# Attention scores of a two-layer decoder from two 12-bit pieces in one-pass matmuls of 32 rows, four heads at once, with maxima added by PE and dense fillers in the loops

## The reference

```python
# layer 0, x: (8, 128, 128), 16 heads of 8
q = q * cos + rotate_half(q) * sin          # 16 wide: two halves of 8
k = k * cos + rotate_half(k) * sin
attn1 = jnp.einsum('bhid,bhjd->bhij', q1, k1) * scale
attn2 = jnp.einsum('bhid,bhjd->bhij', q2, k2) * scale
probs = jax.nn.softmax(attn1, axis=-1) - lam * jax.nn.softmax(attn2, axis=-1)
out = jnp.einsum('bhij,bhjd->bhid', probs, v)          # v is 16 wide
# layer 1, 16 heads of 8, causal
score = jnp.einsum('bhsd,bhtd->bhst', q, k)
attn = jax.nn.softmax(jnp.where(causal, score, -inf) / sqrt(8), axis=-1)
y = jnp.einsum('bhst,bhtd->bhsd', attn, v)
```

## Time and profile before

| | |
|---|---|
| median of 3 runs | 631.55 us (631.34 to 631.91) |
| the profiled execution | 630.57 us, its span 628.8 us |
| mean granted clock of PE | 0.825 |
| busy, share of the span | PE 88%, DVE 43%, ACT 36%, POOL 13% |
| DMA | 31.66 MB, mean 50 GB/s |

### The profile page before, as it was taken

One profiled execution on the slowest core, in us unless ns is written; L12 is line 12 of the kernel. 1 busy time (PEld: TensorE's weight loads), 2 busy tenths in 40 slices (PEclk: granted clock), 3 DMA queues, 4 the chain that ended last, 5 costly groups with the idle time before them and its releaser, 6 DMA issues.

```text
span 628.8 us, 12335 instructions
## 1 busy us (share of the span) xinstructions
PE 553.6 (88%) x4854; PEld 401.8 (64%) x4854; DVE 272.6 (43%) x679; ACT 223.5 (36%) x406; POOL 84.0 (13%) x131
## 2 busy tenths in 40 slices
PE   8658999999886899828999859999999899999994
PEld 3446777777664389415566636677777667677764
DVE  4333444442147643503243359666672325223325
ACT  1202433433323142000245426665665062443340
POOL 4000111111131000200000044322222100000001
PEclk9755555555588699955599979999999998999998
DMA  7522221200303000122110000000100000111110
GB/s 224 199 102 100 89 71 69 74 33 2 134 1 134 1 2 2 40 96 100 68 39 24 34 11 10 13 11 11 44 1 1 1 25 23 46 34 34 35 41 33
DMA packets 22637, 31.66 MB, mean 50 GB/s; under 512 B 5428, under 2 KB 13956, under 8 KB 22336
## 3 DMA queue, kind: packets, MB, share of 16 engines
q1 hardware_dynamic: 22592, 31.01, 14.7%
HBM read 26.68 MB, written 4.12 MB: 49 GB/s over the span
## 4 chain that ended last, share of the span: by engine, by line
PE 76%; DVE 12%; DMA 6%; ACT 3%; issue 1%; POOL 1%; SPq 0%; POOLq 0%; DVEq 0%; ACTq 0%
PE ps L563 16%; PE ps L942 9%; PE ps L925 9%; PE ps L585 7%; PE ps L841 4%; PE ps L558 4%; PE ps L598 3%; PE ps L814 2%; PE ps L913 2%; DMA near<-stacks 2%; DMA stacks<-arena 2%; PE ps L822 2%; PE ps L830 2%; PE ps L749 2%; PE ps L783 2%; PE ps L864 2%
## 5 line engine op out<-in xcount | busy, mean ns | idle before, releaser
L1241 DVE TENSOR_REDUCE negm<-ps 128x4 f32<-128x512 f32 x96 | 61.9, 686 | 124.1 <-PE ps L563 124.1
L990 ACT ACTIVATE probs<-ps 128x512 f32<-128x512 f32 (+1 forms) x100 | 56.5, 590 | 97.6 <-PE ps L563 97.2
L563 PE MATMUL ps<-near 8*128 8x128 f32 (+1 forms) x768 | 76.7, 420 | 13.0 <-DMA near<-stacks 6.9
L563 PEld LDWEIGHTS ps<-near 8*128 8x128 f32 (+1 forms) x768 | 65.9, 309 | 28.5 <-issue 22.8
L563 PE MATMUL ps<-w1a 8*128 8x128 f32 (+1 forms) x768 | 69.4, 385 | 0.0
L942 PEld LDWEIGHTS ps<-w1a,arena 128*128 128x128 f32 x512 | 61.0, 196 | 7.2 <-issue 6.2
L990 ACT ACTIVATE arena<-ps,w1a 128x512 f32<-128x512 f32 x64 | 43.4, 687 | 60.6 <-PE ps L925 59.4
L563 PEld LDWEIGHTS ps<-w1a 8*128 8x128 f32 (+1 forms) x768 | 59.2, 277 | 8.4 <-issue 8.4
L1550 DVE SCALAR_TENSOR_TENSOR racc<-ps,sm,racc 128x128 f32<-128x128 f32 x128 | 36.0, 344 | 64.7 <-PE ps L942 64.6
L942 PE MATMUL ps<-w1a,arena 128*128 128x128 f32 x512 | 61.4, 280 | 0.8 <-DVE racc L1541 0.8
L925 PE MATMUL ps<-xT,w1a 128*128 128x512 f32 x128 | 57.9, 594 | 1.4 <-ACT xT L990 1.4
(11 more groups left out here) (180 smaller groups left out, 725.3 us busy)
## 6 DMA issues: line engine op xcount, KB each, us to landing
near<-stacks SPq DMA_DIRECT2D x24, 256.0 KB
w1a<-stacks SPq DMA_DIRECT2D x24, 256.0 KB
stacks<-arena SPq DMA_DIRECT2D x6, 512.0 KB
w1a<-in_w1a SPq DMA_DIRECT2D x1, 2048.0 KB, 7.7
w2a<-in_w2a SPq DMA_DIRECT2D x1, 2048.0 KB, 7.8
w1a<-in_w1b SPq DMA_DIRECT2D x16, 128.0 KB, 2.0
w1a<-in_w2b SPq DMA_DIRECT2D x16, 128.0 KB, 2.1
con<-in_con SPq DMA_DIRECT2D x1, 644.0 KB, 5.7
```

The costliest lines, as they stand in the source:

```text
L563: last = mm(o[:, cols], left[rows, cols], right[rows, cols], start=not causal, stop=not causal or k == 3)
L990: return nc.scalar.activation(o, i, f, **kw)
L1241: nc.vector.tensor_reduce(negm[:, n % 2, 4 * g:4 * g + 4], tiles(bank(RING_S[(4 * n + g) % 3]), 4, P), AX.X, ALU.max, negate=True).then_in ...
```

## The change

Queries and keys are split on DVE and POOL into a high piece (the bits kept by `HEAD_BITS`) and the rest. Two pieces of the queries times two of the keys times 8 dimensions make 32 rows of contraction, stored to and loaded from DRAM accordingly; the operands get the type float32r, for which a matmul is one instruction. A unit v is now four heads of four batches of one half (`place`): 16 units and 8 units as before, with 16 tiles each. The loads of a unit are three DMAs (one for keys, two for queries) and not two, in other lists, and the move of the maxima by DMA is gone: DVE and POOL split the maxima too (`high_maxima`, `split_maxima`), PE transposes the pieces, ACT copies them to `mT` (128 partitions), and for each turned tile a second float32r matmul of 32 rows adds them, with `pick` as weights. Three fillers of 512 columns stand in each step ahead of the first half of `head_values`; the fillers in front of the loops grow from 6 to 8 and from 18 to 30. The two softmaxes of the first attention are now combined in its second half of units, in POOL operations of 256 elements instead of 128.

The core of the diff:

```diff
-MROW = HD
+PIECES = 2
+HEAD_BITS = -4096
 RING = 8
-AHEAD = FLIGHT = 4
-LOADS = 2
+LOADS = 3
...
+            def load_stacks(a, v, count):
+                c, m, half = place(v, count)
+                at = 4 * HD * m * ROW + (2 * c + half) * HALF
+                slot, signal = v % RING, a.stack[v % RING]
+                sp.dma_start(keys_of[slot].bitcast(F32), bass.AP(stacks, KEYS + 4 * HD * m * ROW + at, [[ROW, 8 * HD], [0, 2], [1, HALF]])
+                             ).then_inc(signal, 16)
+                for p in range(PIECES):
+                    sp.dma_start(queries_of[slot][p:P:2, :].bitcast(F32), bass.AP(stacks, p * P * ROW + at, [[ROW, 4 * HD], [0, 2], [1, HALF]])
+                                 ).then_inc(signal, 16)
-                    sp.dma_start(tile, bass.AP(stacks, (t * NH + h) * HEAD, [[HALF, 4], [ROW, QUAD], [1, HALF]])
-                                 ).then_inc(a.stack[h % FLIGHT], 16)
-            def move_maxima(a, n, slot):
-                sp.wait_ge(a.mc, n + 1)
-                sp.dma_start(queries_of[slot][MROW:MROW + 3 * QUAD + 1:QUAD, :], mT[:, n % 2, :]
-                             ).then_inc(a.mrow[n % FLIGHT], 16)
...
+            def low_piece(a, n, turn):
+                pool.wait_ge(a.hi, turn)
+                nc.gpsimd.tensor_tensor(rope[:, 2 * n, :], rope[:, 2 * n, :], rope[:, 2 * n + 1, :], ALU.subtract
+                                        ).then_inc(a.qlo, 1)
+            def split_maxima(a, v):
+                pool.wait_ge(a.mhi, v + 1)
+                nc.gpsimd.tensor_tensor(mparts[:, v % 2, :, 16:32], over(negm[:, v % 2, :], 4), mparts[:, v % 2, :, 0:16],
+                                        ALU.subtract).then_inc(a.msplit, 1)
...
                 for k in range(4):
                     cols = slice(k * P, (k + 1) * P)
-                    for o, left, right, g, depth, _, done in cells:
-                        rows = slice(QUAD * g, QUAD * g + depth)
-                        last = mm(o[:, cols], left[rows, cols], right[rows, cols], start=not causal, stop=not causal or k == 3)
-                        if k == 3:
+                    for o, left, right, g, shift, _, done in cells:
+                        rows = slice(QUAD * g, QUAD * g + QUAD)
+                        last = mm(o[:, cols], left[rows, cols], right[rows, cols], start=not causal,
+                                  stop=shift is None and (not causal or k == 3))
+                        if k == 3 and shift is None:
                             last.then_inc(done, 1)
+                    for o, left, right, g, shift, _, done in cells:
+                        if shift is not None:
+                            rows = slice(QUAD * g, QUAD * g + QUAD)
+                            last = mm(o[:, cols], pick[rows, k, :], shift[rows, :], start=False, stop=not causal or k == 3)
+                            if k == 3:
+                                last.then_inc(done, 1)
...
             def head_maxima(a, n):
-                pe.wait_ge(a.max, 4 * n + 4)
+                pe.wait_ge(a.msplit, n + 1)
...
-            def head_values(a, n, pair, c):
+            def head_values(a, n, part):
...
+                    keep_busy(3, BANK_V)
...
                     if turned:
-                        pe.wait_ge(a.mrow[n % FLIGHT], (a.turns + n // FLIGHT + 1) * 16)
+                        pe.wait_ge(a.mc, n + 1)
...
-            keep_busy(6, BANK_M0)
+            keep_busy(8, BANK_M0)
...
-            keep_busy(18, BANK_M0)
+            keep_busy(30, BANK_M0)
...
+                def high_maxima(n):
+                    dve.wait_ge(a.max, 4 * n + 4)
+                    if n >= 2:
+                        dve.wait_ge(a.mt, n - 1)
+                    ts(mparts[:, n % 2, :, 0:16].bitcast(I32), over(negm[:, n % 2, :], 4).bitcast(I32), HEAD_BITS, None,
+                       ALU.bitwise_and).then_inc(a.mhi, 1)
...
                     if n >= 2:
                         finish_head(n - 2, n % 2)
+                    if 0 <= n + 2 < count:
+                        high_maxima(n + 2)
```

More of the change, by code:

```diff
@@ L18 @@
 BF16 = mybir.dt.bfloat16
+F32R = mybir.dt.float32r
+I32 = mybir.dt.int32
 ALU = mybir.AluOpType
@@ L128, in decoder_kernel @@
         rw0 = sb("rw0", [P, E0])
+        with nc.sbuf_tensor("late", [P, 2, 4, HALF], F32R) as late:
+            pass
         w1a = sb("w1a", [P, E0, F0 * P])
@@ L137, in decoder_kernel @@
         rw1, rb1, b2s = sb("rw1", [P, E1]), sb("rb1", [P, E1]), sb("b2s", [E1, P])
-        near = sb("near", [P, 2, 4, HALF])
-        late = w1a[:].rearrange("p e f -> p (e f)").rearrange("p (k s t) -> p k s t", k=2, s=4)
+        near = sb("near", [P, 2, 4, HALF], F32R)
+        pick = sb("pick", [P, 4, P], F32R)
         probs = sb("probs", [P, 2, 16, P])
@@ L336, in heads @@
[L336 to L349, removed]
@@ L363, in _ @@
             load(w2a[:], d["w2a"], ld_f)
[L364 to L369, removed]
+            for p, (queries, keys) in enumerate(((D.hi, D.hi), (D.qlo, D.klo))):
+                sp.wait_ge(queries, 1)
+                sp.dma_start(bass.AP(stacks, p * P * ROW, [[T, P], [1, T]]), rope[:, 1 - p, :]).then_inc(D.kept, 16)
+                sp.wait_ge(keys, 2 - p)
+                sp.dma_start(bass.AP(stacks, KEYS + p * ROW, [[2 * ROW, PAIRS * HD], [T, 2], [1, T]]), rope[:, 3 - p, :]
+                             ).then_inc(D.kept, 16)
+            sp.wait_ge(D.kept, 16 * 4)
+            heads(D, 0, PAIRS, PAIRS)
             def weights(pair, slot):
@@ new lines, in heads @@
+            def heads(a, count):
+                pool.wait_ge(a.vall, 4 if a is A else 2)
+                split_maxima(a, 0)
+                split_maxima(a, 1)
+                for n in range(count + 2):
+                    if n < count:
+                        if n >= 2:
+                            pool.wait_ge(a.pv, n - 1)
+                        values(a, n, count)
+                    if n + 2 < count:
+                        split_maxima(a, n + 2)
+                    if a is A and n - 2 >= NH // 2:
+                        add_outputs(n - 2)
@@ L615, in step @@
                     if 0 <= n - 1 < count:
-                        head_values(a, n - 1, pair, 0)
+                        head_values(a, n - 1, 0)
                     scored = n + 3 < count
@@ L622, in step @@
                     if 0 <= n - 1 < count:
-                        head_values(a, n - 1, pair, 1)
+                        head_values(a, n - 1, 1)
                     if 0 <= n + 2 < count:
@@ L1056, in _ @@
                 values(g)
+            act.wait_ge(lam_sum, 1)
+            fn(lams[:, 2:4], lams[:, 0:2], ACT.Exp).then_inc(lam_exp, 1)
+            act.wait_ge(ld_p, 16)
+            fn(pick[:], pick_in, ACT.Copy).then_inc(tables, 1)
             for half in range(2):
@@ L1324, in _ @@
             rotate(2)
-            sum_keys(2)
+            dch.wait()
+            dve.wait_ge(A.mul, 3)
+            link(tt(rope[:, 4, :], rope[:, 4, :], rope[:, 5, :], ALU.subtract))
+            high_piece(A, 2)
+            dve.wait_ge(A.full, 1)
+            high_piece(A, 0)
+            low_keys(A, 2, 1)
             rotate(3)
-            sum_keys(3)
+            dve.wait_ge(A.full, 2)
+            high_piece(A, 1)
             dve.wait_ge(ld_l, 16 * 6)
```

238 lines of the change are left out of this document (135 added, 103 removed).

## The result

| | before | changed |
|---|---|---|
| median | 631.73 us (631.34 to 641.25, 4 runs) | 579.37 us (579.21 to 582.12, 4 runs) |
| ratio | | 0.9183, 95% interval 0.9149 to 0.9218 |
| profiled span | 628.8 us | 577.6 us |
| mean granted clock | 0.825 | 0.919 |

The change made the kernel 52 us faster. The forecast was 563 (548 to 606), its likeliest case's own range 553 to 578, so the measured time lies just above that range and inside the wide one. The clock rose in both loops, as that case had it, but 16 us of its gain of 68 did not come. Executions more than 1.5% over the quickest one of the same kernel count as slow and are left out of every ratio here.

What follows compares the result with a forecast made beforehand. PE was taken to bound both head loops. From the profiled 630.6 us, 55.5 came off in the first loop and 13 in the second, giving 562, so 563 us in the median; range 548 to 606.

Steps and rivals of the forecast that it cites:

- likeliest case: Whole kernel: clock up in both loops, score calls of 0.66 to 1.10 us, 553 to 578 us; chance 0.60.
- What bounds: Both head loops: PE alone bounds the steps, full for 7.40 us in the first, with DVE 3.53 and ACT 3.03.
- the rival of an engine other than PE: Steps: DVE, POOL and ACT bound them at about 5.0 to 5.2 us, +10 to 573 us; chance 0.09.
- A float32r matmul: Score calls: 0.85 us instead of 1.10 at the high clock level, 1.3 instead of 2.02 at the low one.
- The clock: Both loops: rises to the high level within the first two steps and stays up; full steps 4.4 us in the first.
- both misses: Within the forecast's range: calls 0.25 us longer cost +8 us, the clock rising two steps later +6 us.
- Start: First loop: loads ready at 31.2, first scores at 31.5, ramp of 8 us, turned scores at 39.5, against 50.81: -11.3 us.
- Second loop: Masks start 4.2 us earlier, ramp -6.0, steps 0 and 1 -3.5, later steps +0.7: sum -13 us.
- one-pass matmuls run one behind another: Score calls: 1152 matmuls not beside each other, at 57 ns instead of 35, +25 to 588 us; chance 0.05.
- a float32r tile is as long as a whole f32 tile: Score calls: 2.0 us each, +1.15 for some 36 calls, +41 to 605 us; chance 0.10.
- the slower case of 112 ns each: Score calls: float32r tiles neither overlap nor are shorter than f32 instructions, +89 to 652 us; chance 0.03.
- The clock staying down in the first loop: First loop: low clock level throughout, steps of 7.4 us again, 604 us; chance 0.08.

Runs made afterwards that it cites:

- Run 8: Changed kernel with each score matmul of the queries' side written twice in the first loop, 32 instead of 24 per full call: 582.32 us.
- run 1: Changed kernel without the three fillers in each step: 607.65 us, ratio to before 0.959.
- run 9: Changed kernel with fillers behind score calls in ramps and first steps, 58 instead of 30 ahead of the second loop, none in later full steps: 546.77 us.
- run 3: Changed kernel with rows of float32r and bf16 test matmuls replacing the 30 fillers ahead of the second loop: 585.04 us, no comparison.
- run 2: Kernel before the change with the same three fillers added in each step: 609.71 us, ratio 0.9621.
- run 12: Kernel before the change with the fillers of run 9, 46 instead of 18 ahead of the second loop: 635.04 us, ratio 0.9951.
- run 4: Changed kernel with three more fillers behind every score call of both ramps and 58 instead of 30 ahead of the second loop: 568.79 us.
- run 5: The kernel of run 4 without the three fillers in the steps of the second loop: 562.97 us, ratio 0.8862.

## Why the prediction came out as it did

- **What bounds** (right). PE is full in every window of full steps, before and after; DVE has 3.3 a step and ACT 2.9. The hop over POOL stays hidden, the rival of an engine other than PE fell.
- **A float32r matmul** (the mis-sized term). I took "0.85" for a call at the high level "nearest for the pace of instructions", inside bounds of 0.66 and 1.10; it is 1.04, and 1.90 at the low level against my 1.3. Run 8 shows why the pace of 34 ns was the wrong row: it is what four row groups make of 0.11 to 0.13 each, not a rate of instructions. The right row was 3.57/32 = 0.112 of the earlier trace rows, by eight in one row group, which I had as the upper bound. So the call saves 0.06 of 1.10, not 0.25. A step was 4.73 and not 4.4: +3.9 us over twelve steps, +0.9 in steps 14 and 15, and +2.8 in the second loop's steps behind the first two (+0.44 each in place of +0.18): 7.6 in all.
- **The clock** (right that it rises, wrong when: the step that failed). "I take it to rise within the first two steps of both loops": it fell in the ramp and was back only within the third step of the first loop (at about 58) and at the end of step 1 of the second. In the first loop steps 0 and 1 took 13.1, not 10.3, the third 2.8 more than the steps behind it, and in the second loop steps 0 and 1 took 19.2, not 14.5: 10.3 us in all (the low level's longer calls among them). The working had priced both misses, a call 0.25 longer at +8 and a clock two steps later at +6; they came together, which put the time 1 us beyond that case's range. "Every cell uses all 32 rows" as a ground for the rise was wrong (run 1: 0.50 for 90 us); "fillers of 128 rows" was right. And "stay up, as the step of 6.22 does" was right, even without fillers (run 9).
- **Start** (right, too careful). First scores at 30.07 where I had 31.5. Right ahead of them in the chain stand PE's own fillers (28.34 to 30.07), which I had ending at 31.4; the loads, waited for before, no longer are. In lists of 64 or 32 outer entries they reach a share of 0.90, against 0.27 before, as the rule of the Trainium skill (DMA: Bandwidth & Descriptors, why a DMA increments its semaphore by 16) had it. The ramp was 8.5 for 8.0, turned scores at 38.59 for 39.5.
- **Second loop** -5.0 (predicted -4.2) before the masks, -4.8 (-6.0) in the ramp, +1.1 (-3.5) in steps 0 and 1, +3.5 (+0.7) behind: -5.2 in place of -13. The first loop gave -46.1 in place of -55.5.
- **The rivals.** That one-pass matmuls run one behind another, that a float32r tile is as long as a whole f32 tile, and the slower case of 112 ns each all fall to run 3. The clock staying down in the first loop, 604, is what run 1 shows for the kernel without its fillers: 607.65.

What the change is made of, by the ratios of runs 1 and 2: 26 us from the scores and DMAs without the fillers, 24 us from the fillers without the scores, 52 from both. The shorter matmuls are a small part (0.06 of a call at the high level, 0.12 at the low one). Better placed fillers bring 33 us more with the new operands and loads (run 9) and hardly any with the old ones (run 12), where PE idles ahead of both loops and again for the maxima's DMA. That these waits, and not the 8-row matmuls, are the reason is argued, not shown. The change as made collects 52 of 85 us: its fillers stand in the full steps, where they are needed only because the level was lost before, and none stands where it is lost (ramps, step 0).

## What to carry to other kernels

Price a row-group matmul by the number that stand one behind another in one row group and by the length of one in a row, not by instructions per time over all groups: half-idle groups make the average look fast. Spend fillers where PE waits (a ramp, the first steps, ahead of a loop) and take them out of steady steps, then look whether the clock holds. Look first for waits on another engine or a DMA. A long one ahead of a loop made the same fillers useless, and behind a recurring one with a microsecond of idle PE an otherwise full PE stood at half the level for the rest of the loop (run 12), where three fillers in each step brought it back by 108 us after a fall at 105 (run 2).

## What the runs showed of the hardware that I had not expected

- The level depends on how a stretch was entered: the same steps with PE full stood at 0.50 for 90 us (run 1) and at 1.00 (run 9). When it comes back differs between executions: with the same first loop at about 63.6 us (run 4) and at 55 (run 5).
- A float32r matmul of 128 columns takes 0.129 us in a row, one of 512 only 0.246; bf16 0.056 for 128 columns.
- DVE and POOL hold each other up in the split at the start. The changed kernel in order of time:

```profile
22.31 0.68 DVE L1347 TENSOR_SCALAR arena<-arena 128x1024 int32<-128x1024 int32 x1
...
22.47 2.72 POOL L460 TENSOR_TENSOR arena<-arena 128x1024 f32<-128x1024 f32 x1
...
22.91 2.31 DVE L1408 TENSOR_TENSOR lamin<-lamin 128x16 f32<-128x16 f32 x1
...
25.15 2.35 POOL L466 TENSOR_TENSOR arena<-arena 128x1024 f32<-128x1024 f32 x1
...
25.34 2.71 DVE L1347 TENSOR_SCALAR arena<-arena 128x1024 int32<-128x1024 int32 x1
```

The bit-wise operation takes 0.68 in one place and 2.71 in another, where it began just behind a POOL operation of 2.35; an operation of 16 elements a row took 2.31 and ended when POOL's did. The Trainium skill (Trainium Architecture — The Big Picture, what this means for kernel authors) says that the pair's shared port is locked, not divided, and these rows agree. In the kernel before, with POOL idle beside it, the operation of 16 elements took 0.17 (at 21.02); no run took POOL's work away from the bit-wise one.
